# Delta rule: one 128-column product for transitions and reads, with the masked products stored over the values

## The reference, cut to what matters

```python
def step(W, inp):
    q_t, k_t, v_t, b_t = inp
    pred = jnp.einsum('bhij,bhj->bhi', W, k_t)
    err = v_t - pred
    W_new = W + b_t[..., None, None] * jnp.einsum('bhi,bhj->bhij', err, k_t)
    o_t = jnp.einsum('bhij,bhj->bhi', W_new, q_t)
    return (W_new, o_t)
```

## Time and profile before

| | us |
|---|---|
| median of 3 runs | 1597.56 (1596.67 to 1597.82) |
| profiled execution, its own time | 1596.03 |
| span in its trace | 1594.2 |
| PE busy | 1433.5 (90% of the span) |
| DVE busy | 1132.2 (71%) |
| ACT busy | 923.1 (58%) |
| POOL busy | 713.8 (45%) |

### The profile page before, as it was taken

How to read it: one execution, slowest core, us unless ns; L and a number is a source line. 1 busy time by engine, 2 the same in 40 slices (tenths; PEclk the granted TensorE clock), 3 DMA queues, 4 the chain that set the end, 5 groups by cost and what they waited for, 6 DMA issues and landing times.

```text
span 1594.2 us, 45033 instructions
## 1 busy us (share of the span) xinstructions
PE 1433.5 (90%) x19640; PEld 811.7 (51%) x19640; DVE 1132.2 (71%) x2307; ACT 923.1 (58%) x1301; POOL 713.8 (45%) x750
## 2 busy tenths in 40 slices
PE   8888888899989899998988988989999999999996
PEld 4222223344444335343434544777887888875453
DVE  6778877898977885868727668576777766474654
ACT  2787776788867776887672433555455544441220
POOL 2124131576756665676670107467776666010000
PEclk9999999999999999999999999999999999989898
DMA  4000003333322341332301000000000002000000
GB/s 166 1 1 1 1 1 108 99 102 91 95 78 78 92 109 57 98 91 78 95 16 70 1 1 14 16 17 17 4 17 17 17 4 92 3 2 1 8 7 14
DMA packets 32421, 70.84 MB, mean 44 GB/s; under 512 B 5329, under 2 KB 7057, under 8 KB 31969
## 3 DMA queue, kind: packets, MB, share of 16 engines
q1 hardware_dynamic: 32224, 67.98, 14.7%
HBM read 47.45 MB, written 20.51 MB: 43 GB/s over the span
## 4 chain that ended last, share of the span: by engine, by line
PE 56%; DVE 17%; ACT 16%; issue 7%; POOL 4%; ACTq 0%; DVEq 0%; POOLq 0%
PE ps L160 54%; ACT b_X L988 4%; ACT a_E L470 3%; DVE b_mx L926 2%; POOL b_EL L1006 2%; ACT b_EH L169 2%; DVE a_MX L433 1%; POOL d_XI L1814 1%; ACT b_Hk L842 1%; PE ps L242 1%; POOL d_tmp L1811 1%; DVE X L234 1%; DVE b_rd L1099 1%; DVE st L172 1%; DVE b_Lq L172 1%
## 5 line engine op out<-in xcount | busy, mean ns | idle before, releaser
L1006 POOL TENSOR_TENSOR b_EL<-b_X,b_EH 128x1024 f16<-128x1024 f32 x160 | 341.6, 2135 | 189.1 <-ACT b_EH L169 188.9
L988 ACT ACTIVATE b_X<-ps 128x1024 f32<-128x1024 f32 x160 | 163.7, 1023 | 86.8 <-PE ps L160 86.6
L1811 POOL TENSOR_TENSOR d_tmp<-d_G,d_XI 128x31 f32<-128x31 f32 (+15 forms) x248 | 127.7, 515 | 157.4 <-DVE d_G L1740 138.6
L433 DVE TENSOR_REDUCE a_MX<-ps 128x2 f16<-128x1024 f32 x128 | 155.1, 1227 | 44.7 <-PE ps L160 44.3
L169 ACT ACTIVATE b_EH<-b_X 128x1024 f16<-128x1024 f32 x160 | 169.1, 1057 | 27.0 <-PE ps L160 15.8
L160 PE MATMUL ps<-b_M,b_S 128*64 128x512 f16 (+1 forms) x1408 | 177.2, 384 | 3.3 <-ACT b_X L988 3.2
L926 DVE TENSOR_REDUCE b_mx<-ps 128x2 f32<-128x1024 f32 x128 | 155.7, 1217 | 28.8 <-PE ps L160 27.0
L470 ACT ACTIVATE a_E<-ps 128x1024 f32<-128x1024 f32 x128 | 131.3, 1026 | 49.5 <-PE ps L160 49.5
L1814 POOL TENSOR_TENSOR d_XI<-d_XI,d_tmp 128x31 f32<-128x31 f32 (+15 forms) x248 | 139.3, 562 | 19.4
L160 PEld LDWEIGHTS ps<-b_M,b_S 128*64 128x64 f16 (+1 forms) x1408 | 70.5, 109 | 83.9 <-ACT b_X L988 19.8
L452 POOL TENSOR_TENSOR a_QS<-a_QS,a_MR 128x512 f16<-128x512 f16 x16 | 18.5, 1157 | 183.6 <-ACT a_MR L169 179.7
(11 more groups left out here) (336 smaller groups left out, 3298.1 us busy)
## 6 DMA issues: line engine op xcount, KB each, us to landing
b_S<-s_xk SPq DMA_DIRECT2D x48, 336.0 KB, 6.4
b_M<-s_xq SPq DMA_DIRECT2D x48, 256.0 KB, 5.1
s_xk<-b_Hk SPq DMA_DIRECT2D x16, 336.0 KB, 2.2
s_xk<-b_Lk SPq DMA_DIRECT2D x16, 336.0 KB, 2.5
s_xq<-b_Hq SPq DMA_DIRECT2D x16, 256.0 KB, 2.0
s_xq<-b_Lq SPq DMA_DIRECT2D x16, 256.0 KB, 2.0
d_XI<-eye SPq DMA_DIRECT2D x8, 512.0 KB, 3.5
f_w<-f_w SPq DMA_DIRECT2D x1, 2048.0 KB, 8.6
```

The lines of the kernel that those rows point to most:

```text
L433: v.e.tensor_reduce(out, PS[:, bk:bk + 2, :], AX, ALU.max).then_inc(sem("a_mx"), 1)
L988: a.e.activation(b_X[k % 2], PS[:, bk:bk + 2, :], ACT.Exp, scale=0.125).then_inc(sem("b_ex"), 1)
L1006: last = p.e.tensor_tensor(b_EL[k % 6], b_X[k % 2], b_EH[k % 6], ALU.subtract)
L1811: e.tensor_tensor(tm, a, x, ALU.mult).then_inc(*p.step())
```

## The change

`transitions` and `reads` have the same stationary operand (the 64 columns of `d_UW` from X times the keys). The new `spread(p)` multiplies it in one product of 128 columns by [masked products | keys], which lie side by side in `d_KV`, because VectorE now writes the masked products over the values there. Since the values are read by the four solves, the masks wait for `d_um` of the last solve, and `products()` moves from ahead of the solves to behind them. `update("do")` reads the masked products from `d_KV`. VectorE's subtractions for `d_AT` and `d_QT` are made per pair of heads p and half: eight instructions in place of six. The semaphores `d_a` and `d_qq` count to four per unit.

```diff
             def keys_of(r, p, c, par):
                 return KV[r, c, 1, 4 * j + head(p, par), :]
 
-            def transitions(r, p, c, par):
-                return U[r, at_chunk(p, c, par), 64:128], keys_of(r, p, c, par)
-
-            def reads(r, p, c, par):
-                i = at_chunk(p, c, par)
-                return U[r, i, 64:128], P[r, i, :]
+            def spread(p):
+
+                bk = [ringD.take(t, ("dr", u, p, half), 1, "d_qq", 4 * u + 2 * p + half + 1) for half in range(2)]
+                t.wait_ge("d_u", 4 * u + 4)
+                t.wait_ge("d_pt", 2 * u + 2)
+                for k, c, half, par in TILES:
+                    if k == p and 2 * c + half > 0:
+                        r, n = HALF[half], 2 if 2 * c + half < 7 else 1
+                        last = mm(e, PS[HALF[par], bk[half], 128 * c:128 * c + 64 * n], U[r, at_chunk(p, c, par), 64:128],
+                                  KV[r, c, 0:n, 4 * j + head(p, par), :])
+                last.then_inc(sem("d_rm"), 1)
...
             fold()
             yield
-            products()
             yield
             for k in range(4):
                 solve(k)
                 yield
-            yield
-            update("da", "d_a", "d_am", 64, 128, 1, 6, transitions)
+            products()
             yield
             update("db", "d_b", "d_bm", 64, 128, 0, 6, steps)
             yield
-            yield
-            t.wait_ge("d_pt", 2 * u + 2)
-            update("dr", "d_qq", "d_rm", 256, 64, 1, 7, reads)
+            for p in range(2):
+                spread(p)
+                yield
             yield
             update("do", "d_o", "d_om", 256, 64, 0, 7, outputs)
             yield
...
+            for _ in range(8):
+                yield
             v.wait_ge("d_ptm", u + 1)
+            v.wait_ge("d_um", 4 * u + 4)
             for par in range(2):
...
+                e.tensor_tensor(KV[:, :, 0, 4 * j + par:4 * j + 4:2, :].rearrange("p c a n -> p a c n"),
+                                PS[:, bank["dp", u, par], :].rearrange("p (a c n) -> p a c n", a=2, c=4),
+                                d_mu.unsqueeze(1).unsqueeze(1).broadcast_to([128, 2, 4, 64]), ALU.mult).then_inc(sem("d_pt"), 1)
+                yield
...
+            for p in range(2):
+                v.wait_ge("d_rm", 2 * u + p + 1)
+                for half in range(2):
+                    o = 1 - half
+                    ps = PS[:, bank["dr", u, p, half], :].rearrange("p (c k n) -> p c k n", c=4, k=2)
+                    e.tensor_tensor(A[:, o:o + 3, half, p, :], d_id.unsqueeze(1).broadcast_to([128, 3, 64]), ps[:, o:o + 3, 1],
+                                    ALU.subtract).then_inc(sem("d_a"), 1)
+                    x = q[:, p, o:4, half, :]
+                    e.tensor_tensor(x, x, ps[:, o:4, 0], ALU.subtract).then_inc(sem("d_qq"), 1)
+                yield
             yield
...
-                    streams.append((later(9, split(lane)), 18))
+                    streams.append((later(13, split(lane)), 22))
```

More of the change, by code:

```diff
@@ L1978, in d_prep_scalar @@
                      PS[:, bank["db", u, half], 0:128 * n].rearrange("p (c n) -> p c n", c=n)).then_inc(sem("d_b"), 1)
-            yield
+            for _ in range(2):
+                yield
             yield
@@ L2022, in d_prep_vector @@
-            v.wait_ge("d_am", u + 1)
-            A = d_AT[j].rearrange("p (c k) a n -> p c k (a n)", k=2)
-            for half in range(2):
-                o = 1 - half
-                ps = PS[:, bank["da", u, half], 128 * o:128 * o + 384]
-                for a in range(2):
-                    last = e.tensor_tensor(A[:, o:o + 3, half, 64 * a:64 * a + 64], d_id.unsqueeze(1).broadcast_to([128, 3, 64]),
-                                           ps.rearrange("p (c a n) -> p c a n", c=3, a=2)[:, :, a], ALU.subtract)
-                last.then_inc(sem("d_a"), 1)
@@ L2031, in d_prep_vector @@
-            yield
-            yield
-            yield
-            v.wait_ge("d_rm", u + 1)
-            q = d_QT[j].rearrange("p a (c k n) -> p a c k n", c=4, k=2)
-            for half in range(2):
-                o = 1 - half
-                x = q[:, :, o:4, half, :]
-                ps = PS[:, bank["dr", u, half], :].rearrange("p (a c n) -> p a c n", a=2, c=4)
-                e.tensor_tensor(x, x, ps[:, :, o:4], ALU.subtract).then_inc(sem("d_qq"), 1)
-            yield
+            for _ in range(8):
+                yield
```

22 lines of the change are left out of this document (8 added, 14 removed).

## The result

The changed kernel takes **1631.42 us** (median of 5 runs, 1627.58 to 1636.02), the kernel before, run beside it, 1596.91 us (5 runs, 1592.38 to 1597.82): a ratio of **1.0238, 95% interval 1.0213 to 1.0264**. It is slower by 34.5 us; forecast were 17. The profiled execution has a span of 1625.8 us against 1594.2.

The account below looks back on a forecast made before the run. TensorE's stream with its gaps was taken to bound each pass. Terms: 8.25 (passes like 3), 2.7 (4, 8), 0.75 (2, 6, 10), 0.5 (11), 4.5 (12 to 14): +16.7 us, 1614 us likeliest, range 1602 to 1627.

Parts of the forecast that it names:

- The two waits of TensorE on VectorE: TensorE waits for the masks, 1.25 us in pass 3, and for the subtraction freeing a spread's bank, 1.6 us.
- The gaps closed: TensorE's issue gap, 1.1 to 1.3 us a pass, read as late instruction supply, closes with fewer products.
- Products behind the solves gain nothing ahead of them: Ahead of the solves, the products' 0.93 us turn into a wait for ScalarE's copy of `fold`.
- 128-column records at 27 ns: In the spreads, four quadrants overlap, so a 128-column record takes 27.5 ns and a spread 0.72 us.
- Passes 1, 3, 5, 7, 9: Five passes like pass 3, each +1.65 us from the waits for masks and bank: 8.25 us.
- Up to the key products at 1149.34 nothing moves: In pass 4, TensorE waits there for ScalarE's copies and the moved products fit into that wait: no added time.
- Passes 2, 4, 6, 8, 10 otherwise: Mask and bank waits: passes 4 and 8 +1.35 us each; 2, 6, 10 +0.25 each, having no layer-norm rows there.
- Unit 0 and pass 0 at 0: Preparation of unit 0 and pass 0 lose nothing, since they wait for other things as well: 0 us.
- Passes 11 to 13 at +3.5: Pass 11, without keys, +0.5 us; pass 12 with layer norm and 13 with attention rows on VectorE, 1.5 each.
- Pass 14 at +1.5: Attention rows on VectorE stand in front of the subtraction; estimate 1.5 us by pass 4's size.
- only the mask wait: Rival: VectorE subtracts in time, outputs do not wait for the bank; -0.4 us in pass 3, 1591 us; chance 0.08.
- part 3: The forecast's timeline of pass 3 after the change: mask wait 1.25 us, outputs' wait 1.6, `d_wo` 1.65 later.

Follow-up runs that it names:

- e11: Changed kernel with eight extra 256-column matmuls per unit put into TensorE's wait for the masks: 1637.79 us, ratio 1.0285.
- e14: Changed kernel with VectorE's subtractions from both spreads one place earlier in its order: 1623.32 us, ratio 1.0188.
- e7: Kernel before with the merge into 128 columns only; products and masks stay ahead of the solves, masks write `d_PT`: 1602.60 us, ratio 1.0046.
- e1: Changed kernel with a third buffer for the turned keys `d_KT`: 1628.06 us, ratio 1.0219.
- e12: The changed kernel run again unchanged, for a second trace: 1634.98 us, ratio 1.0257.
- e2: Changed kernel with the outputs between the two spreads, ScalarE's copy and VectorE's first subtraction moved along: 1625.54 us, ratio 1.0204.
- e3: Changed kernel with the products between second and third solve for units 0 to 13, each mask waiting only for the solves it needs: 1620.72 us, ratio 1.0178.
- e4: Changed kernel with products between second and third solve and outputs between the two spreads: 1617.94 us, ratio 1.0150.
- e6: Kernel before with only the products and their masks moved behind the solves, nothing merged: 1617.19 us, ratio 1.0141.
- e5: Kernel before with eight extra 256-column matmuls per unit between reads and outputs: 1615.03 us, ratio 1.0109.
- e8: Kernel before with the merge only, products early, and the outputs between the two spreads: 1602.72 us, ratio 1.0048.
- e9: Kernel before with eight extra 256-column matmuls per unit ahead of the reads: 1611.20 us, ratio 1.0109.
- e10: Merge with early products; steps, spreads, ScalarE's copy of the steps and VectorE's subtractions one place earlier: 1612.93 us, ratio 1.0116.
- e13: Merge with early products, and on VectorE alone the subtractions from both spreads one place earlier: 1595.56 us, ratio 1.0015.

## Why the prediction was wrong

The direction was right and the two waits of TensorE on VectorE came about as forecast; the sum was half of what was measured, because one path was left out and several terms were too small. In the loop the trace has +38.9 us, the sum +16.7. Of the 22.2 us between them, rounded, 6.2 belong to the step that failed, 4.0 to the other terms of the even passes, 2.3 to the odd passes, 1.2 to the clock in pass 4, 2.7 to unit 0 with pass 0, 1.3 to passes 11 to 13 and 4.6 to the stretch from pass 14 on. The steps:

- **The two waits of TensorE on VectorE**: right. L2019 14.2 us in 15 waits, forecast "near 15"; L2034 16.0 in 12. e11 shows the first to be dead time. The second is dead time in the odd passes and pass 12: e14 takes away all but 0.3 us of it and is 8 to 12 us faster, and the even passes from 2 to 10 gain nothing.
- **The gaps closed**: right. Forecast was that no issue gap of over 0.5 us is left between steps and projection; one is, 0.87 us in pass 10, the other eight rows of that name being the wait for the copy of `fold`.
- **Products behind the solves gain nothing ahead of them**: right in the passes, first solve 2.57 us behind `fold` in both kernels; not in unit 0, below. **128-column records at 27 ns**: right (0.7 us a spread; e7's cost has no slow pairs in it). **Masks with strides at today's price**: right; the group's mean is 688 ns, 683 before.
- **Passes 1, 3, 5, 7, 9**: forecast +8.25, measured +10.5 (22.35 against 20.49 us in pass 3). A small miss.
- **"Up to the key products at 1149.34 nothing moves"**: this is the step that failed. It asked only whether TensorE's work fits into ScalarE's wait. ScalarE's first copy of turned keys also waits until the products of the unit in preparation have read the buffer it overwrites; with the products early that was always so, with them late the copy starts only behind them (2.97 us of standing still in pass 4), and the solve's copy is queued behind it. The key products start 11.15 us behind `fold` instead of 9.75. e1 shows its price: 6.2 us over passes 2, 4, 6, 8 and 10 (155.6 to 149.4). With it the sum would have been some 1620.
- **Passes 2, 4, 6, 8, 10 otherwise**: forecast +3.45, measured +14.8 with 6.2 from the failed step and 1.2 from the clock in pass 4 (33.39 against 32.17 in e12), so some 7.4 are left for the two waits. In e1 passes 4 and 8 are 1.9 and 2.1 us longer than before (forecast 1.35 each), passes 2, 6 and 10 0.7, 0.3 and 2.3 (forecast 0.25 each). Why pass 10 loses so much more than 2 and 6 is open.
- **Unit 0 and pass 0 at 0**: +2.7. Unit 0 has no chain's step beside it, and the first solve's wait for the copy of `fold`, which the products covered, is bare there. The solves of unit 0 now, then before:

```profile
1015.07 5.27 PE L160 MATMUL ps<-d_KV,d_XE 64*64 64x128 f32 x62 [1.38 <-ACT d_XE L169]
```

```profile
1018.42 3.71 PE L160 MATMUL ps<-d_KV,d_XE 64*64 64x128 f32 x64 [0.29 <-ACT d_XE L169]
```

  Behind the wait of 1.38 us the clock falls to half for a part of the time: it is 0.80 on the mean from 1014 to 1017 us and 0.63 from 1017 to 1020; in the kernel before it stays at 1.00, and the solves take 3.71 us instead of 5.27. From unit 0's `fold` to the next one the clock is 0.93 in all traces with the products behind or between the solves (after, e1, e2, e3, e4, e6, e11, e12, e14) and 1.00 in all with them ahead (before, e5, e7, e8, e9, e10, e13). In pass 0 it is 0.94 or 0.95 in every kernel but before, e5 and e9, so there the merge alone is enough; why is not shown. With late products these two windows lose 2.7 to 3.8 us together, with early ones at most 1.5.
- **Passes 11 to 13 at +3.5**: +4.8, and +3.2 in e12. Pass 12 has a clock of 0.94 in the first trace and 1.00 in e12 (27.87 and 26.30 us).
- **Pass 14 at +1.5**: from pass 14 on +6.1 and +7.4 in the two traces, at a clock of 0.91 and 0.87, before 0.90. TensorE stands still for 11.1 and 10.5 us there, before for 5.1. The waits around unit 15 are 2.1 us for the masks and 4.8 in two for the bank (2.28 and 2.51). The term was worked out by pass 4's size. There VectorE has only work of its own in front of the subtraction; here it stands still behind a row of the attention, which itself waits for TensorE:

```profile
1452.94 0.75 DVE L2321 TENSOR_SCALAR e_Qp<-ps,e_bxy 128x512 f32<-128x512 f32 x1 [3.64 <-PE ps L160]
```

Of the rivals, "only the mask wait" decided from a VectorE 1.6 us earlier at the subtraction. e14 makes that so in the changed kernel, and the time is 1623.32, not 1591: the price of this rival was wrong. Its -0.4 us a pass leaves out that the products' 0.93 us now stand uncovered behind the solves; by the times of part 3 the outputs without the bank's wait end at 1132.4, where they ended at 1132.35 before, which is no gain. e14's passes 5 and 9 bear that out, with 20.75 and 20.74 us against 20.31 and 20.56. Only where the products stay early (e13) does the same order on VectorE bring the merge level with the kernel before.

## What to carry to other kernels

A step that is moved later is late for everyone who waits for it as a reader too: list each semaphore that it increments and every wait on it, the ones that protect a buffer from being overwritten above all, and then what is queued behind each of those waits. Merging products gains only what the engine's own stream loses (here 9 us of gaps), and one bank more held for another engine can bring twice that in waits. Where a wait for another engine's instruction comes up, look first at what stands in front of that instruction in its own order: one place on VectorE took 19.3 us of waits to 1.9 and won 7 us of time, while moving TensorE's side as well made another wait (e10). Count a wait as won only after looking pass by pass at what ends last without it. And read the profile's name for a wait together with its place: eight gaps called "issue" were the wait for one copy.

## What the runs showed of the hardware

- In the first trace of the changed kernel TensorE's granted clock fell to half (1.2 of 2.4 GHz) in pass 4, after two waits of 1.44 and 1.76 us within 6 us in which it was busy for 4.09:

```profile
1160.00:1166.00 6.00, 4.09 (x189) 3.93 (x193) 3.85 (x13) 3.09 (x4) 0.00 (x0) 1.00 0.02 4
1166.00:1169.30 3.30, 3.30 (x71) 3.18 (x71) 3.30 (x8) 0.35 (x1) 0.00 (x0) 0.50 0.02 5
```

  The outputs took 1.97 us instead of 1.16, and the pass 33.39 instead of 32.17. The second trace has the same waits in this pass (e12: 1.4 and 1.8 us) at a clock of 1.00. So the same program is or isn't throttled there, and a drop in one trace need be no property of the kernel; the drop behind unit 0's `fold`, which stands in every trace with the products behind or between the solves, is one.
- A right operand whose two halves lie some 14,000 to 26,000 words of 4 bytes apart costs a 64x128 product nothing: 28 records of a spread take 0.99 us in e7 and in the changed kernel, where the halves are 512 words apart, and the mean record 276 ns in both.
